# Splitting W2's seven sums beside the attention instead of in the changeover to the feed-forward

## What is computed

```python
q, k, v = x @ Wq + bq, ctx @ Wk + bk, ctx @ Wv + bv          # heads of 32
scores = where(j < i, q @ k.T / sqrt(32), -1e30)
attn = softmax(scores); attn[:, :, 0, :] = 0
x = layer_norm(x + (attn @ v) @ Wo + bo, ln1_g, ln1_b)
ffn = relu(x @ W1 + b1) @ W2 + b2
out = layer_norm(x + ffn, ln2_g, ln2_b)
```

## Time and profile before

| | us |
|---|---|
| median of 3 runs | 2703.1 (2698.96 to 2703.62) |
| the profiled execution | 2702.73 |
| its span in the profile | 2700.9 |
| PE busy | 2618.1 |
| DVE busy | 2095.5 |
| POOL busy | 1577.6 |
| ACT busy | 1527.2 |

### The profile page before, as it was taken

One profiled execution on the slowest core, in us unless ns is written; L12 is line 12 of the kernel. 1 busy time (PEld: TensorE's weight loads), 2 busy tenths in 40 slices (PEclk: granted clock), 3 DMA queues, 4 the chain that ended last, 5 costly groups with the idle time before them and its releaser, 6 DMA issues.

```text
span 2700.9 us, 61812 instructions
## 1 busy us (share of the span) xinstructions
PE 2618.1 (97%) x22604; PEld 2238.3 (83%) x22604; DVE 2095.5 (78%) x4723; ACT 1527.2 (57%) x2945; POOL 1577.6 (58%) x1724
## 2 busy tenths in 40 slices
PE   7999999999999999977999999999999999999998
PEld 5888888888888888765888888888888888888887
DVE  6888888888888888878776767677767676767675
ACT  4777777777777777767434344444444444434443
POOL 3777777766766666656554545555555555555553
PEclk9999999999999999987999999999999999999999
DMA  7556555655555555555423232313232222222220
GB/s 198 150 147 156 151 146 141 159 152 137 150 138 133 138 138 132 140 138 157 95 49 71 49 70 50 69 49 71 50 69 51 68 52 68 52 67 54 65 52 28
DMA packets 439553, 273.33 MB, mean 101 GB/s; under 512 B 299648, under 2 KB 334400, under 8 KB 439248
## 3 DMA queue, kind: packets, MB, share of 16 engines
q1 hardware_dynamic: 438288, 267.79, 39.9%
q10 hardware_dynamic: 960, 1.57, 0.3%
HBM read 109.86 MB, written 57.67 MB: 62 GB/s over the span
## 4 chain that ended last, share of the span: by engine, by line
PE 75%; DVE 11%; issue 5%; SPq 3%; POOL 3%; DMA 2%; ACT 1%; ACTq 0%; DVEq 0%; POOLq 0%
PE h_ps L1368 21%; PE acc L1384 19%; PE lin_ps L707 9%; PE front L1354 6%; PE lin_ps L703 5%; PE max_ps L682 4%; PE st_ps L729 4%; PE o_ps L749 3%; POOL prob_lo L422 2%; PE o_ps L751 2%; DVE max_ps L660 2%; SPq L846 2%; PE st_ps L764 2%; DVE xT L509 1%; DMA x_in<-in_x 1%
## 5 line engine op out<-in xcount | busy, mean ns | idle before, releaser
L422 POOL TENSOR_TENSOR prob_lo<-probs,prob_hi 128x512 f16<-128x512 f32 (+1 forms) x768 | 789.0, 1042 | 403.0 <-ACT prob_hi L501 401.0
L1368 PE MATMUL h_ps<-x_halves,W 128*128 128x256 f16 x6144 | 756.5, 273 | 1.1 <-ACT hf L1182 1.1
L1384 PE MATMUL acc<-W,hs 128*128 128x256 f16 x5376 | 669.5, 273 | 1.0 <-DVE hs L1328 1.0
L1368 PEld LDWEIGHTS h_ps<-x_halves,W 128*128 128x128 f16 x6144 | 596.6, 98 | 87.4 <-issue 14.3
L1182 ACT ACTIVATE hf<-h_ps,b1s,scale_evac 128x256 f32<-128x256 f32 x512 | 284.5, 562 | 562.2 <-PE h_ps L1368 560.2
L1384 PEld LDWEIGHTS acc<-W,hs 128*128 128x128 f16 x5376 | 525.9, 98 | 62.3 <-issue 1.5
L499 ACT ACTIVATE probs<-st_ps 128x512 f32<-128x512 f32 (+1 forms) x768 | 407.1, 530 | 287.1 <-PE st_ps L764 250.3
L660 DVE CUSTOM_DVE_ANT_0 max_ps<-max_ps,mask_q 128x256 f32<-128x256 f32 (+2 forms) x768 | 421.7, 563 | 137.1 <-PE max_ps L682 136.8
L1108 POOL TENSOR_TENSOR hf<-hf 128x256 f32<-128x256 f32 x256 | 240.0, 938 | 482.0 <-ACT hf L1182 481.4
L501 ACT ACTIVATE prob_hi<-st_ps 128x512 f16<-128x512 f32 (+1 forms) x768 | 408.2, 531 | 0.0
L1328 DVE TENSOR_TENSOR hs<-hf,hs 128x896 f16<-128x896 f32 x256 | 282.9, 1124 | 148.5 <-ACT hs L1171 148.4
(11 more groups left out here) (122 smaller groups left out, 3842.3 us busy)
## 6 DMA issues: line engine op xcount, KB each, us to landing
heads<-stage SPq DMA_DIRECT2D x756, 128.0 KB, 2.4
raw<-in_xT SPq DMA_DIRECT2D x64, 256.0 KB, 3.1
o_in<-ctx_rows SPq DMA_DIRECT2D x256, 64.0 KB, 2.7
x_in<-in_x SPq DMA_DIRECT2D x32, 512.0 KB, 4.0
x_rows<-x SPq DMA_DIRECT2D x64, 256.0 KB, 2.0
o_in<-x_rows SPq DMA_DIRECT2D x256, 64.0 KB, 2.4
out<-y SPq DMA_DIRECT2D x32, 512.0 KB, 3.1
raw<-in_cT SPq DMA_DIRECT2D x60, 256.0 KB, 3.4
```

Of the source, the lines that this page charges most:

```text
L422: pool.tensor_tensor(prob_lo[:, k % 4, 0:w], probs[:, k % PROBS, 0:w], prob_hi[:, k % 4, 0:w], ALU.subtract).then_inc(pl_done, 1)
L1368: last = pe.matmul(h_ps[:, f % 2, 0:T], W1[:, aw, j, f * P:(f + 1) * P], x1_halves[:, item.parity, aa, j, :], start=(j == 0 and m == 0), s ...
L1384: last = pe.matmul(acc_products[:, n, :], hs[:, p % HS, aa, n, :], W2[:, p, aw, n, :], start=(p == 0 and m == 0 and n % 2 == 0), stop=(p = ...
```

## The change

For each pair the seven blocks are split in the attention, right after POOL has made the sums. In place of one scale for the whole of W2 there is a power of two for each row (partition) of a pair, made from the scan's result by four small DVE steps in slot 50. ACT makes the high half in slots 54 (the three sums, 768 elements in each partition, into the new tile `mix_hi`) and 60 (the other four blocks, 1024 elements, into `raw` itself), DVE the low half in slots 55 and 61. The halves go to `w2_halves`, in float16: two DMAs from SP in slot 56 and two from ACT in slot 62, in place of the three of `mixed_w2`. The context loads of the next item move from slots 14 to 17 to slots 19 and 20, and the small row loads (`heads<-rows`) stand ahead of them in SP's list.

In feed-forward W2 comes ready-made in eight DMAs from ACT's queue, two in slot 7, two in 13, three in 19 and one in 22. Only W1 is split, one chunk per slot from slot 5 to slot 20. The row factors are taken back in the ReLU's scale and bias (`h_evac`, one column per pair, and `b1s`), for which DVE has three more small steps. In memory the seven blocks lie in another order (`BLOCK`). The matmuls are the same in number and shape.

```diff
 # Bounds
-        self.mixed_w2 = nc.dram_tensor("mixed_w2", [P, self.pairs, 7, 256], F32, kind="Internal").ap()
+        self.w2_halves = nc.dram_tensor("w2_halves", [P, self.pairs, 2, 7, 256], F16, kind="Internal").ap()
...
+    def mixes(self, raw):
+        block = raw[:, :, :].rearrange("p i (h n) -> p (i h) n", n=256)
+        half = raw[:, :, :].bitcast(F16).rearrange("p i (h n) -> p (i h) n", n=512)
+        return block, ((block[:, 4:7, :], self.mix_hi[:, :, :], half[:, 4:7, 0:256]),
+                       (block[:, 0:4, :], half[:, 4:8, 256:512], half[:, 0:4, 0:256]))
 # attention
-    CTX_LOAD = 14
+    CTX_LOAD = 19
-    MIX_STORE = SLOTS + 11
+    HALF_HI = (SLOTS + 6, SLOTS + 12)
+    HALF_LO = (SLOTS + 7, SLOTS + 13)
+    HALF_STORE = (SLOTS + 8, SLOTS + 14)
...
+    def store_halves(eng, item, g, at):
+        _, parts = bounds.mixes(raw)
+        for part, ready in ((0, bounds.half_hi), (1, bounds.half_lo)):
+            wait_for(eng, ready, 2, item, g + 1)
+            eng.dma_start(bounds.w2_halves[:, item.n, part, at, :], parts[g][1 + part]
+                          ).then_inc(bounds.halves_stored, 16)
 # attention, scalar
+                        if g == 0:
+                            wait_for(act, bounds.row_step, 4, item, 4)
+                            wait_for(act, bounds.halves_stored, 64, item, 0)
+                        else:
+                            wait_for(act, bounds.half_lo, 2, item, 1)
+                        wait_for(act, bounds.mixed, 5, item, (3, 5)[g])
+                        act.activation(hi, src, ACT.Copy, scale=bounds.row_value[:, 1:2]).then_inc(bounds.half_hi, 1)
+                for item, _ in due(window, s, SLOTS, B, HALF_STORE[1]):
+                    if item.n < bounds.pairs:
+                        store_halves(act, item, 1, slice(0, 4))
 # attention, vector, after the scan
+                        dve.tensor_scalar(value, bounds.part[:, :], 1e-12, None, ALU.max).then_inc(bounds.row_step, 1)
...
+                        dve.tensor_scalar(power.bitcast(U32), value.bitcast(U32), 0x7F800000, None, ALU.bitwise_and
+                                          ).then_inc(bounds.row_step, 1)
...
+                        dve.reciprocal(value, power).then_inc(bounds.row_step, 1)
...
+                        dve.tensor_scalar(scale, value, SUM_TOP, None, ALU.mult).then_inc(bounds.row_step, 1)
+                for g in range(2):
+                    for item, _ in due(window, s, SLOTS, B, HALF_LO[g]):
...
+                        dve.scalar_tensor_tensor(out=lo, in0=src, scalar=bounds.row_value[:, 1:2], in1=hi,
+                                                 op0=ALU.mult, op1=ALU.subtract).then_inc(bounds.half_lo, 1)
 # feed, scalar
+                for p in range(PAIRS):
+                    if (window, s) == (W2_LOAD[p] // SLOTS, W2_LOAD[p] % SLOTS):
+                        act.wait_ge(*(before.heads_read + [before.o_read])[heads_group(p)])
+                        act.wait_ge(bounds.halves_stored, 64 * PAIRS)
+                        if heads_group(p) == 4:
+                            for i in range(2):
+                                act.wait_ge(early.stored[i], before.row_stores * (CHUNKS // 2))
+                        act.dma_start(W2[:, p, :, :, :], bounds.w2_halves[:, p, :, :, :]).then_inc(w2_loaded[p], 16)
 # feed
-        return n if n < KT else PROJ + (n - KT) * 2 // 3
+        return n if n < KT else PROJ + n - KT
```

More of the change, by code:

```diff
@@ L352, in sync @@
                     load_vectors(sp)
+                for t in range(GROUPS):
+                    for item, _ in due(window, s, SLOTS, B, ROW_AT + 12 * t):
+                        wait_for(sp, rows_ready, GROUPS, item, t + 1)
+                        both = heads[96:98, t, 0, :, :].bitcast(F32).rearrange("p h (q a n) -> p (h q) a n",
+                                                                               a=P // 32, n=32)
+                        for a in range(P // 32):
+                            sp.dma_start(both[:, :, a, :], rows[32 * a:32 * a + 32, t % 2, :]
+                                         ).then_inc(rows_loaded[t % 2], 16)
                 for j in range(KT):
-                    for item, _ in after_first(due(window, s, SLOTS, B, CTX_LOAD + j)):
+                    for item, _ in after_first(due(window, s, SLOTS, B, CTX_LOAD + j // 2)):
                         src = source(cT, item, j)
@@ L428, in gpsimd @@
                             continue
-                        block = raw[:, :, :].rearrange("p i (h n) -> p (i h) n", n=256)
+                        block, _ = bounds.mixes(raw)
                         if n == 0:
@@ L493, in scalar @@
                         split(item, "x", j)
+                for g in range(2):
+                    for item, _ in due(window, s, SLOTS, B, HALF_HI[g]):
+                        if item.n >= bounds.pairs:
+                            continue
+                        _, parts = bounds.mixes(raw)
+                        src, hi, _ = parts[g]
+                        if g == 0:
[6 more added lines that the diff above has]
+                for item, _ in due(window, s, SLOTS, B, HALF_STORE[1]):
+                    if item.n < bounds.pairs:
+                        store_halves(act, item, 1, slice(0, 4))
                 for item, k in due(window, s, SLOTS, B, ST_AT, SLOTS):
@@ L936, in feed @@
         b1s = sb("b1s", [P, FT])
+        h_evac = sb("h_evac", [P, PAIRS])
         stats = sb("stats", [P, 2, U, 6])
@@ L949, in feed @@
     w_lo = sem("w_lo")
-    b1_scaled = sem("b1_scaled")
+    w2_loaded = [sem(f"w2_loaded{p}") for p in range(PAIRS)]
+    h_scales = sem("h_scales")
     bv_hi = sem("bv_hi")
@@ L1017, in part_of @@
     def part_of(n, part):
-        if n >= KT and order[n - KT][0] == "w2":
-            return chunks[n][1][part]
         return chunks[n][1][:, part, :]
-    def raw_of(n):
-        if n >= KT and order[n - KT][0] == "w2":
-            return raw_slot(n).rearrange("p (h n) -> p h n", h=2)
-        return raw_slot(n)
     def weights_due(window, slot, behind=0):
@@ L1035, in feed @@
     scale_w1, scale_w2, scale_x1, scale_h = (bounds.scale[:, n:n + 1] for n in range(4))
-    h_evac, y_evac, y_less = bounds.evac[:, 0:1], bounds.evac[:, 3:4], bounds.less[:, 0:1]
-    weight_scale = [None] * KT + [{"w1": scale_w1, "w2": scale_w2}[w] for w, _ in order]
+    y_evac, y_less = bounds.evac[:, 3:4], bounds.less[:, 0:1]
     acc_products = acc[:, :, :].rearrange("p b (h n) -> p (b h) n", h=2)
@@ L1152, in scalar @@
                         act.wait_ge(bounds.ready, 2)
-                    if n >= KT and order[n - KT][0] == "w2":
-                        act.wait_ge(*(before.heads_read + [before.o_read])[heads_group(order[n - KT][1])])
                     if n < KT:
```

91 lines of the change are left out of this document (49 added, 42 removed).

## The result

The changed kernel takes 2713.4 us (median of 6 runs, 2710.3 to 2716.0), the one before 2703.0: 1.0038 times as long, 95% interval 1.0027 to 1.0050. It is slower by 10.4 us where 2697.0 was forecast, and lies just outside the range. The profiled execution has a span of 2712.2 us against 2700.9, 11.3 us more.

The account below looks back on a forecast made before the run. PE was taken to bound attention and feed-forward, with idle time in the changeover. From the profiled 2702.7 us, minus 12.5 net changeover gain, plus 6.4 attention loss, gave 2696.6, plus 0.4 for the median: 2697.0, range 2682 to 2713.

Parts of the forecast that it names:

- What bounds the kernel: Attention and feed-forward are PE-bound, each PE stall costing its full length; the changeover has 18.9 us of PE idle.
- Gain after the splits' removal (6.5 + 4 + 3): Changeover: 6.5 us from slots 5 to 20, 4 after slot 20, 3 from the clock; 13.5 us saved (3 to 27).
- 0.8 of DVE's share: Changeover, slots 5 to 20: of 8.1 us of DVE work removed, 6.5 us comes back as time.
- The clock term of 3 us: Changeover, 1205 to 1262: fewer PE gaps let part of 31 us run at 2.4 GHz; 3 us (0 to 10).
- Loads of W2 ("0 to 4 us, taken as 0"): Changeover: three W2 loads in a burst may delay the x1 rows by 0 to 4 us, counted as 0.
- First place, small steps (0.5): Attention, between scan and next `max_ps`: four small DVE steps stall PE 0.45 to 1.2 us per batch; 0.5 taken.
- Second place, 768 elements (0.15): Attention, before the group's last `max_ps`: DVE's 768-element split stalls PE 0 to 0.9 us per batch; 0.15 taken.
- Third place (0.15): Attention, slot 14: ACT waits for DVE's second split, then issues two stores; PE stalls 0 to 1.2 us, 0.15 taken.
- Each stall of PE also gives the later steps time to catch up.: Attention: reason for taking 0.8 us per batch, near the low ends; 6.4 us over eight batches (3 to 26).
- the slower rival: Attention: DVE falls behind; PE waits for `max_ps` twice, ACT once; 2.4 us per batch, 2709.6 us; chance 0.22.
- Neither sign of being wrong: A batch length above 75.4 us, or a changeover that is not shorter, would make the prediction wrong.
- Nothing else in the attention: Attention: context loads issued later, from slot 19, cost nothing; the split needing them comes some 7.5 us on.

Follow-up runs that it names:

- change_only: The changed kernel without making W2's halves in the attention, zeros of the same bytes stored from SP instead: 2701.4 us, 0.9992 of the kernel before.

## Why the prediction was wrong, step by step

- **What bounds the kernel.** Right: attention and feed-forward bound by PE, a stall of PE paid in full, the changeover by waits.
- **Gain after the splits' removal (6.5 + 4 + 3).** The step that failed most: "I take 0.8 of DVE's share". The changeover gave 1.7 us in the median with the bursts and about 4 without. Removing 16 more DVE splits was worth about a quarter of their time; by that rate the forecast's 24 us of W2 would have been worth some 5. I had summed what DVE was busy with, and not asked which instruction PE waited for: the longest wait of the earlier trace rows ends with an `onorm` that stands behind the first chunk's layer norm, and did not move (4.7 us before, 4.5 after). PE's idle time in the first stretch was to fall to 12 us or less and was 21.8. The clock term of 3 us came to nothing in the first stretch (0.73 before and after); from 0.97 to 1.00 in the second is 3.5 us fewer at 1.2 GHz, worth at most 1.7.
- **Loads of W2 ("0 to 4 us, taken as 0").** I looked at the burst of three in slot 19 and at when W2 is needed, and named a delay of x1's rows, but took it as nothing without asking what else is in flight. The two loads of slot 13 delayed x1's rows by 5.4 us; the bursts cost 4 us in the runs (1.0038 to 1.0025, and 0.9999 to 0.9984). It stayed inside the bounds of 0 to 6 for this part. Issuing the three of slot 19 took ACT 1.87 us, inside the 1.4 to 2.6, and left it idle for 1.35; what PE lost by that isn't shown.
- **First place, small steps (0.5).** Lag 0.47 as forecast; worth 0.3 to 0.4 when moved.
- **Second place, 768 elements (0.15).** 0.64 measured, inside its bounds of 0 to 0.9. I had written "1.1, or 2.1 when disturbed" and gone by the undisturbed one. It was disturbed 7 times in 7, since every batch repeats the same order.
- **Third place (0.15).** 0.54, inside its bounds, but by another mechanism: not ACT standing before two stores, whose issue took 0.38 us each beside its activations, but DVE's split holding POOL's `prob_lo`.
- **"Each stall of PE also gives the later steps time to catch up."** This was the reason for taking 0.8 us, and little of it holds: the three add up to 0.47 + 0.64 + 0.54 = 1.65 us per batch, 13.2 in eight where 6.4 were forecast. Without the low halves at the second or third place just their own 0.64 or 0.54 went; without the first stall the lag at the second place was 0.84 us in place of 1.11, so 0.2 of the 0.47 was owed later. The 1.65 us are just past the 1.6 from which the slower rival decides, and that rival named the right neighbour, POOL, though it expected two waits for `max_ps`.
- **The range and the signs.** The high end of the gains adds up to 27.7 us and the low end of the attention to 3.6, written as 27 and 3. Neither sign of being wrong that the prediction names came (a batch above 75.4 us, a changeover that is not shorter): both were set so wide that both parts could miss inside them, on the same side.
- **Nothing else in the attention.** Right: later context loads, moved row loads and four stores per pair in place of three cost nothing (change_only, where SP issues all four).

Left open: why one and the same kernel varies by 10 us from run to run, and which of the changeover's remaining waits would have to go for the clock to rise earlier; no run changed the first chunk's layer norm, Wo's splits, the scale chain or the last item's row loads.

## What to carry to other kernels

Where the order of work repeats, contention repeats too: read from the timeline what the neighbour on the shared port does at the very slot in which a new DVE instruction will stand, and price it as disturbed every time or put it where both engines have a gap. Removed work is worth only what it takes away from in front of the instruction that PE waits for, not its sum. And compare the same stage: where one stage grows, move the windows of the next by as much. Before large loads are issued together, look at which small load of another queue is in flight and who waits for it, and issue them one at a time after it.

## What the runs showed of the hardware

- A DVE instruction with two inputs from SBUF and a POOL one hold each other up: 1.02 us alone and 1.72 beside POOL for 768 elements; POOL's 1.16 became 1.69. Three pieces of 256 elements take longer (0.83 each, in slots 10, 11 and 13) than one of 768 (1.36, in slot 10).
- Issuing a single store from ACT took 0.37 to 0.38 us in the median, and ACT's activations overlapped it, as here in the changed kernel:

```profile
334.95 1.16 ACT L524 ACTIVATE raw<-raw,row_value 128x1024 f16<-128x1024 f32 x1
335.99 0.61 ACT L533 ACTIVATE probs<-st_ps 128x512 f32<-128x512 f32 x1
336.25 0.37 ACTq L312 DMA_DIRECT2D w_halves<-raw  x1
336.46 0.62 ACT L535 ACTIVATE prob_hi<-st_ps 128x512 f16<-128x512 f32 x1
```

Several in a row did hold ACT up, in slot 19 of the changed kernel:

```profile
1272.22 1.87 ACTq L1195 DMA_DIRECT2D W<-w_halves  x3
1274.14 0.72 ACT L1205 ACTIVATE W<-raw,scale 128x512 f16<-128x512 f32 x1 [1.35 <-issue]
```

That is 0.62 us for each of three, and 0.87 for each of the six in the earlier trace rows; the price of a lone store can't be read from such a row. The Trainium skill, "DMA: Bandwidth & Descriptors", section "Issuing engines are not separate DMA queues", calls the issue usually small relative to the DMA; these rows agree: the stores landed after a median of 3.6 us and the loads after 6.2.
- Two transfers of 896 KB from ACT's queue delayed SP's 64 KB ones, issued from 1247.59 on, until 1258; the page has 2.4 us as their median landing. The same section of the skill says that DMAs of all engines run on the same 16 and interleave; the 5.36 us here show what that costs the small one.
